# Attention scores from the queries and keys themselves: four heads in four row groups of the array, in place of one stacked matmul per head with high and low parts

## What is computed

```python
# x: (4, 1024, 256); 16 heads of 16; 8 experts of width 1024, two of them per token
q, k, v  = x @ wq.T, x @ wk.T, x @ wv.T                     # per head
q_embed  = softplus(q) * (cos(freqs), sin(freqs))           # 32 numbers per head and position
k_embed  = softplus(k) * (cos(freqs + bias), sin(freqs + bias))
scores   = einsum('bhsd,bhtd->bhst', q_embed, k_embed) / 4
x        = layernorm(x + softmax(scores) @ v @ wo.T)
gates    = softmax(x @ router_w + router_b)                 # top 2 of 8, capacity 640 each
x        = layernorm(x + sum over experts of gate * (gelu(x @ w1 + b1) @ w2 + b2))
```

## Time and profile before

| | before |
|---|---|
| median of 3 runs | 1173.82 us (1173.16 to 1175.28) |
| profiled execution: span | 1170.2 us |
| between that span and the median run | 3.6 us |
| first scores on PE | 53.8 us |
| last scores step starts | 755.5 us |

### The profile page before, as it was taken

One profiled execution on the slowest core, in us unless ns is written; L12 is line 12 of the kernel. 1 busy time (PEld: TensorE's weight loads), 2 busy tenths in 40 slices (PEclk: granted clock), 3 DMA queues, 4 the chain that ended last, 5 costly groups with the idle time before them and its releaser, 6 DMA issues. The chain is left out here.

```text
span 1170.2 us, 15296 instructions
## 1 busy us (share of the span) xinstructions
PE 975.3 (83%) x5541; PEld 570.9 (49%) x5541; DVE 695.9 (59%) x1119; ACT 648.7 (55%) x750; POOL 444.8 (38%) x295
## 2 busy tenths in 40 slices
PE   4597999999998999998999997933378998889870
PEld 2332334444533434533444442422378898889870
DVE  7855275377485267586457642275177656775536
ACT  1276887776776776787776786900123332333224
POOL 3454054053067044048234124034144534444321
PEclk8698999999998999999999998966688988899895
DMA  5597644453646625537626438100434243342228
GB/s 194 180 256 246 155 107 166 108 143 120 154 140 225 154 71 189 115 123 212 164 72 187 107 96 202 46 23 31 160 105 109 48 117 91 105 93 44 23 29 281
DMA packets 72494, 151.85 MB, mean 130 GB/s; under 512 B 9267, under 2 KB 41204, under 8 KB 71632
## 3 DMA queue, kind: packets, MB, share of 16 engines
q1 hardware_dynamic: 52928, 101.59, 32.5%
q0 software_dynamic: 19472, 49.04, 14.7%
HBM read 88.73 MB, written 61.95 MB: 129 GB/s over the span
## 5 line engine op out<-in xcount | busy, mean ns | idle before, releaser
L527 ACT ACTIVATE prob<-spsum 128x1024 f32<-128x1024 f32 x512 | 493.2, 1021 | 177.6 <-PE spsum L665 177.4
L680 PE MATMUL opsum<-prob,val 128*17 128x512 f32 x2048 | 272.2, 603 | 11.3 <-DVE oraw L912 8.8
L665 PE MATMUL spsum<-qst,kst 97*128 97x512 f32 x512 | 157.5, 429 | 15.0 <-issue 9.7
L665 PE MATMUL spsum<-area_q,kst 97*128 97x512 f32 x512 | 156.3, 426 | 2.9 <-issue 2.8
L665 PEld LDWEIGHTS spsum<-qst,kst 97*128 97x128 f32 x512 | 87.8, 192 | 139.3 <-ACT prob L527 98.5
L665 PEld LDWEIGHTS spsum<-area_q,kst 97*128 97x128 f32 x512 | 86.4, 190 | 124.4 <-ACT prob L527 67.6
L448 POOL TENSOR_TENSOR onorm<-oraw,oden 128x512 f32<-128x512 f32 x32 | 45.4, 1418 | 257.1 <-DVE oden L919 257.0
L417 POOL TENSOR_TENSOR square<-raw 128x512 bf16<-128x512 f32 x32 | 59.9, 1871 | 163.5 <-DVE raw L766 163.4
L919 DVE RECIPROCAL oden<-oden 128x256 f32<-128x256 f32 x64 | 112.2, 1753 | 2.2
L1096 POOL DMA_INDIRECT sum_scratch<-eo,add_idx x40 | 62.1, 1553 | 131.3 <-ACT eo L1185 131.3
L1176 ACT ACTIVATE hraw<-hp,b 128x640 f32<-128x640 f32 x64 | 50.9, 796 | 87.0 <-DVE hid L1258 47.4
(11 more groups left out here) (168 smaller groups left out, 1219.0 us busy)
## 6 DMA issues: line engine op xcount, KB each, us to landing
split_scratch<-area_s POOLq DMA_DIRECT2D x56, 512.0 KB, 4.2
kst<-split_scratch SPq DMA_DIRECT2D x45, 512.0 KB, 13.5
area_k<-in_w SPq DMA_DIRECT2D x16, 1024.0 KB, 7.6
qst<-split_scratch SPq DMA_DIRECT2D x24, 512.0 KB, 7.3
area_q<-split_scratch SPq DMA_DIRECT2D x21, 512.0 KB, 7.0
dispatched<-blank POOLq DMA_DIRECT2D x1, 5300.0 KB, 27.3
rows<-dispatched SPq DMA_DIRECT2D x8, 662.5 KB, 4.4
xT<-in_xT SPq DMA_DIRECT2D x4, 1024.0 KB, 16.1
```

The lines of the kernel that those rows point to most:

```text
L527: act.activation(prob[u % NPB][:], spsum[u % NSB][:].rearrange("p a n -> p (a n)"), ACT.Exp, scale=HD ** -0.5).then_inc(s_exp, 1)
L665: ins = pe.matmul(spsum[u % NSB][:, e, :], kst[par][:, j, P * kt:P * (kt + 1)], qst[par][:, j, HALF * qh:HALF * (qh + 1)], start=True, sto ...
L680: ins = pe.matmul(opsum[32 * j:32 * j + HD + 1, :], val[b % 2][:, kt, h0 + j, :], prob[(2 * s + j // 2) % NPB][:, HALF * (j % 2):HALF * (j ...
```

## The change

`emb` itself is stored and read back; nothing is split. It has two buffers now (the write waits for the transfer of unit u-2), the DVE cast and the POOL subtraction go, and a unit is one transfer of 512 KB in place of two. A stack is now 128 partitions, 32 rows for each of the four heads, queries and keys side by side; a group's fill is two transfers of 512 KB and no row of zeros. The four score matmuls are plain fp32 matmuls of 32 rows, each on its own 32 partitions. An fp32 matmul is two weight loads and two matmuls on the engine, an fp32r one is one of each. The row for the maximum is no longer part of the stack: where the flag asks for it, four matmuls of one row are added per step. For that reason the whole group, not its first step alone, now stands twice in PE's program, in a branch with and in one without the maximum.

```diff
-ROWS = 3 * 2 * HD
+ROWS = 2 * HD
...
-        emb = sb("emb", [P, 2, HALF])
-        split = [area_s[:, 4 * HALF * i:4 * HALF * (i + 1)].rearrange("p (s t n) -> p s t n", s=2, t=2)
-                 for i in range(2)]
+        emb = [sb(f"emb{i}", [P, 2, HALF])[:] for i in range(2)]
...
-        qst = [area_q[0:ROWS + 1], sb("qst1", [ROWS + 1, GH, SEQ], F32R)[:]]
-        kst = [sb(f"kst{i}", [ROWS + 1, GH, SEQ], F32R) for i in range(2)]
+        stacks = [area_q[:, 0].bitcast(F32), sb("stacks1", [P, 2, SEQ])[:]]
+        qst, kst = [[stack[:, qk] for stack in stacks] for qk in range(2)]
...
-            eng.wait_ge(s_hi, u + 1)
-            eng.wait_ge(s_split, u + 1)
-            for part in range(2):
-                eng.dma_start(split_d[qk, b, part, 8 * ct:8 * ct + 8, :, HALF * half:HALF * (half + 1)]
...
+            eng.wait_ge(s_emb, u + 1)
+            eng.dma_start(split_d[qk, b, 8 * ct:8 * ct + 8, :, HALF * half:HALF * (half + 1)]
+                          .rearrange("h (d t) n -> (h d) t n", t=2), emb[u % 2]
...
-                for qk, stack, terms in ((0, qst, (0, 0, 1)), (1, kst, (0, 1, 0))):
-                    for r, part in enumerate(terms):
-                        sp.dma_start(stack[par][2 * HD * r:2 * HD * (r + 1)].bitcast(F32),
-                                     split_d[qk, b, part, h0:h0 + GH].rearrange("h r n -> r h n")
-                                     ).then_inc(s_fill[par], 16)
-                zero_row(grp, s_fill[par])
+                for qk in range(2):
+                    sp.dma_start(stacks[par][:, qk],
+                                 split_d[qk, b, h0:h0 + GH].rearrange("h r n -> (h r) n")
+                                 ).then_inc(s_fill[par], 16)
...
-                pool.wait_ge(s_hi, u + 1)
-                pool.tensor_tensor(split[u % 2][:, 1], emb[:], split[u % 2][:, 0].bitcast(F32),
-                                   ALU.subtract).then_inc(s_split, 1)
...
-            def first_step(grp):
+            def group(grp):
...
                 with pe.If(flag > 0):
...
+                    row_maxima(grp)
+                    for s in range(s0, s0 + STEPS):
+                        scores(s, shifted=True)
...
                 with pe.Else():
                     pe.sem_inc(g_full, GEN + 1)
-                    scores(s)
-                    for job in jobs_at(s):
-                        run(job)
-                    if grp:
-                        values(s - 1)
...
+                    for s in range(s0, s0 + STEPS):
+                        if s == TB // 2:
+                            filled(pe, 0)
+                        scores(s, shifted=False)
+                        for job in jobs_at(s):
+                            run(job)
+                        if s:
+                            values(s - 1)
...
-                for pair in range(2):
-                    u = 2 * s + pair
-                    if u >= NSB:
+                cols = slice(HALF * qh, HALF * (qh + 1))
+                for j in range(GH):
+                    rows, u = slice(ROWS * j, ROWS * (j + 1)), 2 * s + j // 2
+                    if j % 2 == 0 and u >= NSB:
                         pe.wait_ge(s_exp, u - NSB + 1)
...
+                    ins = pe.matmul(spsum[u % NSB][:, j % 2, :], kst[par][rows, P * kt:P * (kt + 1)],
+                                    qst[par][rows, cols], start=True, stop=not shifted)
...
-                if u:
-
-                    dve.wait_ge(s_split, u)
-                link(dve.tensor_tensor(emb[:], raw[:].unsqueeze(1).to_broadcast((P, 2, HALF)),
-                                       table[:, :, HALF * half:HALF * (half + 1)], ALU.mult))
-
                 if u >= 2:
                     v = u - 2
                     stored(dve, v // 4, v % 4)
-                tell(dve.tensor_copy(split[u % 2][:, 0], emb[:]), s_hi)
+                tell(dve.tensor_tensor(emb[u % 2], raw[:].unsqueeze(1).to_broadcast((P, 2, HALF)),
+                                       table[:, :, HALF * half:HALF * (half + 1)], ALU.mult), s_emb)
```

More of the change, by code:

```diff
@@ L209, in attention @@
         s_abs, s_soft = sem("s_abs"), sem("s_soft")
-        s_split = sem("s_split")
         s_half = sem("s_half")
@@ L395, in _ @@
         def _(pool):
-            for i in range(2):
-                pool.memset(kst[i][ROWS:ROWS + 1].bitcast(F32), 1.0).then_inc(s_krow, 1)
-                pool.wait_ge(s_krow, i + 1)
+            pool.memset(row_ones[:], 1.0).then_inc(s_krow, 1)
             def clear_slots():
@@ L626, in first_step @@
                     if grp:
-                        values(s - 1)
-                    pe.wait_ge(s_free, sum(len(jobs_at(i)) for i in range(first, s)))
-                    filled(pe, grp)
-                    base = (GEN + 2) * grp
-                    for j in range(GH):
-                        for t in range(TB):
-                            for half in range(2):
-                                m = (j * TB + t) * 2 + half
-                                if base + m:
-                                    pe.wait_ge(g_free, base + m)
-                                pe.matmul(misc[:], qst[par][0:ROWS, j, P * t:P * (t + 1)],
-                                          kst[par][0:ROWS, j, HALF * half:HALF * (half + 1)],
-                                          start=True, stop=True).then_inc(g_full, 1)
@@ L648, in first_step @@
                 with pe.Else():
                     pe.sem_inc(g_full, GEN + 1)
-                    scores(s)
-                    for job in jobs_at(s):
-                        run(job)
-                    if grp:
-                        values(s - 1)
-            def scores(s):
+                    for s in range(s0, s0 + STEPS):
+                        if s == TB // 2:
+                            filled(pe, 0)
+                        scores(s, shifted=False)
+                        for job in jobs_at(s):
+                            run(job)
+                        if s:
+                            values(s - 1)
@@ new lines, in row_maxima @@
+            def row_maxima(grp):
+                par, s0 = grp % 2, STEPS * grp
+                pe.wait_ge(s_free, sum(len(jobs_at(i)) for i in range(first, s0)))
+                filled(pe, grp)
+                base = (GEN + 2) * grp
+                for j in range(GH):
+                    rows = slice(ROWS * j, ROWS * (j + 1))
+                    for t in range(TB):
+                        for half in range(2):
+                            m = (j * TB + t) * 2 + half
+                            if base + m:
+                                pe.wait_ge(g_free, base + m)
+                            pe.matmul(misc[:], qst[par][rows, P * t:P * (t + 1)],
+                                      kst[par][rows, HALF * half:HALF * (half + 1)],
+                                      start=True, stop=True).then_inc(g_full, 1)
+                pe.wait_ge(g_free, base + GEN + 1)
+                pe.transpose(misc[0:GH * TB, 0:P], gneg[:], ident[:]).then_inc(g_full, 1)
+                pe.wait_ge(g_row, 16 * GH * (grp + 1))
+                pe.wait_ge(s_krow, 1)
```

91 lines of the change are left out of this document (42 added, 49 removed).

## The result

The changed kernel is slower. Its median is 1229.1 us (1224.3 to 1229.4, four runs) against 1173.5 us of the kernel before beside it (1171.8 to 1175.3): a ratio of 1.048, 95% interval 1.045 to 1.051. The profiled execution is the fastest of the four, 1224.3 us, with a span of 1222.5 us, 52.3 above that of before.

The account below looks back on a forecast made before the run. PE was taken as the bound, ACT waiting for its scores. Terms 7 + 12 + 18 + 32 - 6 - 8 - 13 = +42 on the 1170.2 us span, plus 3.6 to the median, gave 1217 us; range 1158 to 1330.

Parts of the forecast that it names:

- The jump: PE's jump over the maxima code before each group: one wait for the target's code packet, 16 x 2.0 = +32 us.
- Rival 1: The jump costs nothing, as PE holds four code packets ahead: 1185 us, chance 0.14.
- The block of scores: PE's scores per step become two fully parallel waves, 1.09 us against 1.12: PE wins nothing.
- rivals 3 and 4: Score block: 3, row groups' weight loads go one after another, 1301 or 1386 us, chance 0.17; 4, see rival 4.
- rival 4: Score block: row groups do not stream together; two at a time 1440 us, one at a time some 1850; chance 0.11.
- The quiet steps: Steps without a job: every second one late through ACT, 2.17 us on average against 2.11, 113 x 0.06 = +7 us.
- Steps with a job: Row groups must empty before the job's full-array load, which is exposed: +0.16 x 115 = +18 us.
- Rival 2: Faster: a change of kind costs PE nothing, at a job or at a jump; 1166 or 1159 us, chance 0.20.
- Behind a softplus: Steps behind a "qk" job, where PE waits for ACT: ACT's 0.43 us later start goes through, 28 x 0.43 = +12 us.
- Start: DVE's chain up to the flag gets shorter in units 0, 1 and 2: 3 x 2.07 = -6 us.
- group 1: Group 1's stall on a store queued behind the clearing goes, as queues carry about 3 MB less: -8 us.
- fills: PE's waits before groups 3, 7, 11 and 15 go, as fills are a third of the bytes: -13 us.

Follow-up runs that it names:

- short jump: Changed kernel with PE's untaken branch cut to row maxima and a group's first step, row-maximum removal in steps 2 to 16 left out: 1166.7 us, ratio 0.992.
- short softplus: The short jump version with ACT's two softplus operations on 64 of their 512 columns: 1153.1 us, ratio 0.984.
- bytes put back: The short jump version with each unit stored a second time and four more 512 KB transfers per fill from group 1 on: 1169.4 us, ratio 0.996.

## Why the prediction was right, and where its terms were off

I forecast 1217 us, slower, and 1158 to 1330; 1229 was measured. The direction came from the right term, but its size was too small, and terms for the scores that were too large made up most of the difference.

**The jump: right mechanism, under-sized.** Forecast 16 x 2.0 = 32 us. The jumps last 55.6 us longer (60.2 - 4.7), 3.5 each, of which 45.5 reach the steps, the array still streaming at their start: 42.3 in the groups' last steps (30.7 + 11.6) and 3.2 before the first scores (51.2 against 48.0). And 11.0 are in the groups' first steps (10.5 + 0.5), a term that I did not have: PE waits for the second packet there, and runs slow blocks behind it. The undone jump gave back 57.6 us of the span and 62 of the median. Nor does PE fetch all the code that it passes, against what I had concluded: by my 63 bytes an instruction that would be some 117 packets (an estimate), and it fetched 86, so about half of the passed ones. The step that failed is "one wait for the target's packet, 2.0 us, as it is nearest to one landing". The packet does land 2.1 us after the jump begins (137.88 to 140.00), but PE goes on only 1.4 us after that. Rival 1 is out. By the page "Runtime: NRT & Kernel Launch" of the Trainium skill (Instruction fetch mechanics) PE would hold eight pages of 256 instructions, and a jump over 1,050 would be free; its other sentence, a window of two pages, is what the runs show, since already 275 passed instructions make some jumps wait.

**The block of scores: right.** The records of a block that ACT doesn't hold show four loads and their matmuls within 0.02 us, the other four loads 0.11 and their matmuls 0.53 us behind the first (0.11 of load, 0.43 of a wave). So rivals 3 and 4 are out (one group at a time would have been 1885 us by rival 4's own terms, not 1850). From the scores' load to the values' it is 1.07 us (I said 1.09), 0.86 of it the two waves, and ACT starts 1.20 us after the load (I said 1.19). The factor of 3.07 for four row tiles, which the page "TensorE: Matmul & The Clock Gate" of the Trainium skill has (Measured speedup vs the span model) and which would have made them 1.13 us, does not hold here: the four stream fully side by side.

**The quiet steps: over-sized.** Forecast +7; the short jump has -2.4. Within a stretch of quiet steps they alternate as I said, 2.05 to 2.07 and 2.22 to 2.24 (forecast 2.07 and 2.26). But the late second pair needs a neighbour that is quiet too, and behind a job the step is 2.05, below the 2.11 of before. I multiplied an average over alternating steps by all 113.

**Steps with a job: over-sized.** Forecast +0.16 each, 18 us. Compared step by step, it nearly holds for most jobs: the usual "qk" step went from 3.83 to 3.97 us, "v" and the output projection from 3.84 to 3.98, most router steps from 2.91 to 3.04. A turn step pays 0.09, and "norms", a bf16 job, 0.04 (2.34 to 2.38). That is 8 to 9 us in all, half of the forecast. The table shows nothing for the other jobs because some single steps that were long in the kernel before no longer are, for example "norms" in step 14 of group 10, from 3.98 to 2.38. I took the 1.04 us between scores and a job's matmul from one "qk" step for all 115. Rival 2, that changes of kind cost nothing, is thus wrong for both, the jobs and the jump. Why "norms" pays less was not taken apart.

**Behind a softplus: right.** Forecast 28 x 0.43 = 12; measured 21 x 0.49 = 10.3; the other seven softpluses fall where one group passes into the next and are counted there. The short softplus shows that ACT holds these steps.

**Start, group 1, fills: sizes right, one cause wrong.** The first scores of the short jump are at 48.05, 5.8 us earlier (forecast 6), though step 1 gives 2.8 back (8.70 in place of 5.95). That it came so near is in part luck: with nearly the same start they are at 45.0 to 48.3 us in the other runs built on the changed kernel. Group 1's stall went, -7.8 (forecast -8), and the waits ahead of the groups, -11.6 (forecast -13). I ascribed both to fewer bytes; with the bytes put back they stay away, so that was wrong. The 9 to 10 us of group 14 I did not foresee: in the profiled execution of before, its steps 10 to 13 ran at 2.11 us beside the same transfers, and its last step stood 6.0 us for a fill. As the stall also comes with the old scores, it is no cost of theirs.

In sum for the short jump: scores and jobs +13.2 (-2.4, -0.2, +5.5 with the 2.8 of step 1 in it, +10.3), stalls gone -19.9, group 14 +9.4, start -5.8: -3.1, and -2.2 behind the steps, -5.3 on the span. The forecast without its jump was +10.7. So 16 us too much there stand against 26 too little for the jump (57.6 - 32), and part of what made 1217 near is that they offset each other.

## What to carry to other kernels

Look at what a rare branch makes the common path jump over, on each engine: here a taken jump is free over 155 instructions and costs 3.5 us over 1,050, and it showed in no engine's busy time, only as "issue" before the next matmul. Test the rare case in many small branches (240 of them cost nothing) rather than standing the whole loop twice. And when a change halves bytes, ask what the transfers' start and spread were before counting on it.

## What was not expected of the hardware

A jump's cost is mostly all or nothing: 0.2 to 0.4 us, or 3.3 us and more, with 2.8, 0.8 and 0.7 us where the packet was on its way; the longest was 6.3 us. The second wait follows it at some targets: 2.9 us between the starts of the second and third matmul at group 7. Reads of 4 KB rows into 32 partitions ran at 209 GB/s and into 128 partitions at 311 GB/s on the mean of the same stretch (400 and more at its end), with the DMA engines 90% and 81% busy. A transfer whose outermost extent is 2 moved 50 GB/s. And 16 indirect transfers of 1 us each on POOL's queue can keep PE's signal of finished scores from ACT for up to 6 us, though neither engine has a part in them.
